# A gated cross-attention and expert layer: order of SyncE's loads around the fourth expert, of VectorE's head splits, and four tiles of TensorE's loop written out

## What is computed

```python
x = x + tanh(g_xattn) * attention(ctx, layernorm(x), mask)   # queries from x; keys, values from ctx and x; 4 heads of 64
x = x + tanh(g_ffn) * experts(layernorm(x))                  # top 2 of 8 experts per token, weighted by router probability
# expert(x) = gelu(x @ w1[e] + b1[e]) @ w2[e] + b2[e]        # w1: 256 x 1024, w2: 1024 x 256
```

## Time and profile before

| | |
|---|---|
| timed runs | 896.8, 899.3, 900.4 us; median 899.3 |
| profiled execution, its own time | 906.47 us |
| its span, first to last instruction | 904.7 us |
| mean granted clock of TensorE | 0.987 |
| PE busy | 855.7 us (95%) |
| DVE busy | 645.3 us (71%) |
| ACT busy | 511.5 us (57%) |
| POOL busy | 289.5 us (32%) |

### The profile page before, as it was taken

How to read it: one execution, slowest core, us unless ns; L and a number is a source line. 1 busy time by engine, 2 the same in 40 slices (tenths; PEclk the granted TensorE clock), 3 DMA queues, 4 the chain that set the end, 5 groups by cost and what they waited for, 6 DMA issues and landing times.

```text
span 904.7 us, 19559 instructions
## 1 busy us (share of the span) xinstructions
PE 855.7 (95%) x5968; PEld 657.3 (73%) x5968; DVE 645.3 (71%) x1500; ACT 511.5 (57%) x1371; POOL 289.5 (32%) x241
## 2 busy tenths in 40 slices
PE   3898999999999999999999999899999999999995
PEld 3654555545555455555469999899999999999995
DVE  6766777768777667676897777775755776676695
ACT  2668875787857877468841843443433443353462
POOL 2321212221265212641054238332332322232233
PEclk8899999999999999999999999999999999999998
DMA  4801000130012201120044649352442535362272
GB/s 128 248 1 50 1 1 1 47 96 1 7 54 82 94 1 56 50 94 1 2 137 99 181 82 259 58 144 47 96 90 43 137 72 114 47 145 45 37 230 27
DMA packets 71896, 70.26 MB, mean 78 GB/s; under 512 B 18593, under 2 KB 66977, under 8 KB 71841
## 3 DMA queue, kind: packets, MB, share of 16 engines
q1 hardware_dynamic: 57696, 52.73, 20.0%
q0 software_dynamic: 13152, 16.86, 10.9%
q10 hardware_dynamic: 992, 0.00, 0.1%
HBM read 44.04 MB, written 26.31 MB: 78 GB/s over the span
## 4 chain that ended last, share of the span: by engine, by line
PE 56%; DVE 17%; issue 13%; POOL 8%; ACT 4%; DMA 1%; another core or an unknown queue 0%; SPq 0%; POOLq 0%; DVEq 0%; ACTq 0%
PE psS L1705 22%; PE psF L1901 10%; PE psO L1901 10%; DVE p_sum L1141 6%; PE psS L1822 4%; POOL rr L681 4%; POOL routed L691 3%; PE psO L1838 3%; PE psF L1705 2%; PE psF L1869 1%; ACT sq L828 1%; DMA xr<-in_x 1%; PE psO L1850 1%; DVE Q L1124 1%; PE psO L1705 1%
## 5 line engine op out<-in xcount | busy, mean ns | idle before, releaser
L889 ACT ACTIVATE V<-psS,b_col 128x256 f32<-128x256 f32 x280 | 116.9, 470 | 214.8 <-PE psS L1705 195.3
L699 POOL DMA_INDIRECT out<-V,token_i x70 | 121.5, 1736 | 261.8 <-DVE V L1332 240.5
L872 ACT ACTIVATE p_ring<-psS,shift 128x1024 f32<-128x1024 f32 x128 | 136.6, 1111 | 71.7 <-PE psS L1822 69.7
L681 POOL TENSOR_TENSOR rr<-ssm,minus_half 128x4 f32<-128x4 f32 (+1 forms) x72 | 76.1, 1057 | 282.4 <-DVE ssm L1105 282.4
L1838 PE MATMUL psO<-p_ring,V 128*64 128x512 f32 x576 | 148.5, 612 | 0.0
L1141 DVE TENSOR_TENSOR p_sum<-p_sum,p_ring 128x1024 f32<-128x1024 f32 (+1 forms) x112 | 135.7, 1211 | 1.3
L1901 PE MATMUL psF<-ln_hi,K 128*128 128x256 f32 x560 | 124.2, 285 | 0.2
L1822 PEld LDWEIGHTS psS<-Q,K 64*128 64x128 f32 x864 | 77.0, 187 | 61.3 <-issue 41.9
L1822 PE MATMUL psS<-Q,K 64*128 64x512 f32 x864 | 121.3, 413 | 0.0
L1901 PE MATMUL psO<-ln_hi,K 128*128 128x256 f32 x560 | 120.5, 279 | 0.0
L1309 DVE CAST K<-V 128x512 fp32r<-128x512 f32 x140 | 60.4, 431 | 59.1 <-ACT V L889 57.0
(11 more groups left out here) (297 smaller groups left out, 1766.5 us busy)
## 6 DMA issues: line engine op xcount, KB each, us to landing
xr<-in_L_ffn_w SPq DMA_DIRECT2D x11, 1024.0 KB, 8.2
xn<-in_L_ffn_w SPq DMA_DIRECT2D x11, 1024.0 KB, 5.6
lnf<-routed SPq DMA_DIRECT2D x35, 258.0 KB
routed<-pad_rows SPq DMA_DIRECT2D x17, 258.0 KB, 9.9
xr<-in_x SPq DMA_DIRECT2D x8, 512.0 KB, 4.5
xb<-in_x SPq DMA_DIRECT2D x4, 1024.0 KB, 6.1
out<-xb SPq DMA_DIRECT2D x4, 1024.0 KB
b_raw<-in_L_ffn_b SPq DMA_DIRECT2D x11, 128.0 KB, 3.5
```

The costliest lines, as they stand in the source:

```text
L681: pool.tensor_tensor(rr[0:p, c % 2, n], ssm[0:p, c % 2, n], minus_half[0:p, n], ALU.pow).then_inc(rr_ready, 1)
L699: pool.indirect_dma_start(out_rows, bass.IndirectOffsetOnAxis(ap=token_i[:, m:m + 1], axis=0), y_out[:, m, :], None, bounds_check=NTOK - 1 ...
L872: act.activation(p_ring[0:p, u % RING, :], psS[u % 2][0:p].rearrange("p a n -> p (a n)"), ACT.Exp, bias=bias).then_inc(exp_done, 1)
L889: act.activation(g32[:, q % 2, (c % 2) * TM:(c % 2 + 1) * TM], psH[q][:, (c % 2) * TM:(c % 2 + 1) * TM], ACT.Gelu_apprx_tanh, bias=b1_col[ ...
```

## The change

On SP, the first weights of expert 3 are sent ahead of the last three pads, and its second weights behind the rows of tile 8 and b1. The wait for the whole plan moves behind the loads for tiles 9 and 10; for the rows one part of the plan is waited for. On DVE, `mean_squares(c)` moves ahead of `heads_lo(c-1)` in the groups with `behind` (not i = 0, not the `waited` ones, not i = 6 of windows 3 and 5). `router_softmax` of windows 3 and 5 (i = 4) moves ahead of `scale_heads`; `norm_offsets` of sequence 1 moves from group 5 to group 4; `plan_experts` moves behind `turned_lo(8)` and `take_meta(8)`. On PE, tiles 5 to 8 are written out and the loop starts at 9.

```diff
                     pad(e)
                 load_rows(7, kept_row(7))
+                load_w1(3)
                 for e in range(5, NE):
                     pad(e)
-                load_w1(3)
-                load_w2(3)
                 load_rows(8, kept_row(8))
                 load_b1(3)
+                load_w2(3)
                 sp.wait_ge(scattered, B * (32 * T))
                 sp.wait_ge(pads_filled, 16 * NE)
-                sp.wait_ge(plan_ready, 4)
+                sp.wait_ge(plan_ready, 1)
                 load_rows(KTILES, sp.value_load(tile_row[0:1, KTILES:KTILES + 1], min_val=0, max_val=NE * REGION - TM))
...
                 load_b1(KE + 1)
+                sp.wait_ge(plan_ready, 4)
                 tiles = sp.value_load(tile_count[0:1, 0:1], min_val=SURE, max_val=NTILES)
...
-                    if turned_at(g) is not None and not waited:
+                    routed = not even and past and not last
+                    behind = tile_at(g) is not None and turned_at(g) is not None and not waited and i != 0 and not (routed and i == 6)
+                    if turned_at(g) is not None and not waited and not behind:
                         heads_lo(turned_at(g))
                     if tile_at(g) is not None:
                         mean_squares(tile_at(g))
+                    if behind:
+                        heads_lo(turned_at(g))
+                    if routed and i == 4:
+                        router_softmax(b - 1)
...
-                    if even and more and b == 0 and i == 5:
+                    if even and more and b == 0 and i == 4:
                         norm_offsets(b + 1)
...
                         if i == 4:
-                            router_softmax(b - 1)
                             router_largest(b - 1, 0)
...
                         activate(t, q)
-                    if t == 7:
-                        plan_experts()
...
                         if t == 7:
+                            plan_experts()
                             plan_switches()
...
-                with pe.Fori(5, SURE - 1) as t:
+                for t in range(5, KTILES):
+                    first_layer(t)
+                    turn_tile(t + 1)
+                    second_layer(t)
+
+                with pe.Fori(KTILES, SURE - 1) as t:
```

## The result

The changed kernel took 902.7 us (median of 7 runs, 901.3 to 904.3), the kernel before beside it 899.9 (7 runs, 896.8 to 900.7). The ratio is 1.0031, with a 95% interval of 1.0017 to 1.0045. I had forecast 899.1 us and no change that can be measured. It is slower by 2.8 us: inside my range, short of my bound of 0.5%, and well outside what the interval leaves to chance. The profiled execution of the changed kernel took 904.25 us, with a span of 902.5.

What follows compares the result with a forecast made beforehand. PE was taken to set the end, so edits count only through gaps between its matmuls. From 899.3 us, attention gains of 6.5, attention losses of 6.9 and 0.6 won in the experts gave 899.1 us, range 892.5 to 904.

Steps and rivals of the forecast that it cites:

- the last term of the sum: Experts, tiles 7 to 10: of 8.5 us lost in the profile, 1.3 left to win in timed runs, half taken: -0.6 us.
- The five long turn waits: Attention: PE's waits of 0.75 to 1.00 us before turning heads each shrink by 0.46 us, 2.3 us gained.
- the offsets: Attention, `norm_offsets` moved to group 4: ready before ACT asks, so the turn in group 7 is no longer late; 1.5 us gained.
- the softmax: Attention, windows 3 and 5: `router_softmax` moves into DVE's wait for POOL's 1.12 us; 0.65 us each, 1.3 us gained.
- i = 8: Attention, windows 2, 4 and 6: DVE's split waits behind `ssm` for ACT's squares, PE's transposes start 1.02 us later each time.
- i = 7: Attention, windows 2, 4 and 6: `ssm` waits for squares, the split PE already waits for starts 0.7 us later each time.
- i = 2 of windows 3 and 5: Attention: `turn_norm` needs a split that now ends later, behind `ssm`; 0.7 us lost each, 1.4 us in all.
- window 7: Attention, i = 1: `turn_logits` loses 0.3 us by the same reckoning as `turn_norm`.
- The second rival: Attention: `heads_lo` comes in time for the extra transposes, so gains stand alone: 892.2 us; chance 0.12.
- the third: Attention: bank waits stay, gains fail because late turns follow DVE's total work; only the offsets' 1.5 us kept: 904.7 us; chance 0.13.
- POOL's scatters bind: Experts, tile 9: the last scatter starts at 571.73, later than the plan would be; if it binds anyway, the edits win nothing.
- The first rival: Experts: tile 7's stall is in the timed runs and the edits end it, 8.5 us less: 891.2 us; chance 0.17.

Runs made afterwards that it cites:

- late heads put back: Changed kernel, but DVE takes the heads' low half in the old order in nine groups of windows 2 to 7; 896.07 us, ratio 0.9951 to the kernel before.
- scatters early: Changed kernel, but POOL sends the last sequence's scatters in two eights ahead of the adds of tiles 5 and 6; 903.05 us, ratio 1.0025 to the kernel before.
- the wait filled: Changed kernel, but PE turns the identity 28 times ahead of its wait for tile 9's rows; 899.83 us, ratio 1.0000 to the kernel before.
- late heads put back, SP's order of before: Changed kernel with the heads' low half in the old order in nine groups and SP's order as before; 893.48 us, ratio 0.9927 to the kernel before.
- late heads put back, wait filled: Changed kernel with the heads' low half in the old order in nine groups and 28 identity turns before tile 9's rows; 893.12 us, ratio 0.9922 to the kernel before.
- the last experiment: Changed kernel, but expert 3's second weights leave ahead of tile 8's rows, as in the kernel before; 900.43 us, ratio 1.0012 to the kernel before.

## Why the prediction was wrong

**The step that failed** is the last term of the sum, "What of the 8.5 us is in a timed run? ... -0.6 us". I took what the edits do in tiles 7 to 10 for a small gain. Less what the attention gained in the profile (0.65 us), they cost about 3.5 us in the first measurement (medians 899.9 and 902.7) and 2.4 in the second (900.4 and 902.1). Two things were left out.

The first is a wait. I had written that "the rows of tile 9 can't be sent before 573 or so, and the turn of tile 9 is due at 575.7", and stopped there. I gave the last scatter only its 1.10 us on POOL; the rows left 4.5 us behind its start, at 576.10, and PE had them another 3.4 us later, where I had put nothing. About a microsecond of this is the change's own: with only some of its parts the rows leave 3.3 to 3.5 us behind that start. So PE, with tiles 7 and 8 undisturbed, came early to rows that come late, and stood 4.37 us. For the most part that is the old loss moved.

The second is the clock. I counted a standstill by its own microseconds and left out what it does to the tile behind it: 2.2 us. The Trainium skill has this mechanism ("TensorE: Matmul & The Clock Gate", section "HAM oscillation — how this bites in real kernels"): a wait for a DMA between bursts of matmuls lowers the clock, and the burst behind it starts slow. The traces here agree: 14.07 us for a tile of 11.84. I had weighed a rule on instruction fetching and not this one, which spoke against the change.

| in the profile, tiles 7 and 8 | longest wait of PE, us | half clock there, us | clock's cost in the timed runs, us |
|---|---|---|---|
| kernel before | 1.6 | 3.4 | 7.7, 7.5 and 7.0 (35, 30, 23 runs) |
| the same, again | 1.6 | none | 8.4 |
| SP's edits alone | 1.2 | none | 8.4 |
| attention edits alone | 0.7 | none | 9.1 |
| all but SP's edits | 0.7 | none | 7.9 |
| written out only | 1.0 | none | 7.6 |
| changed kernel | 4.4 and 4.6 | 6.8 and 6.9 | 10.6 and 9.6 |
| late heads put back | 4.0 | 3.4 | 9.6 |
| scatters early | 1.9 | 3.4 | 10.1 |
| second weights ahead of tile 8's rows | 3.1 | 3.4 | 8.9 |
| the wait filled | 1.6 | none | 6.8 |
| late heads put back, SP's order of before | 1.3 | none | 7.6 |
| late heads put back, wait filled | 1.8 | none | 6.9 |

The last column scatters by half a microsecond and more (the copy of the kernel before stands at 8.4, its runs beside it at 7.7), and the attention edits alone, at 9.1, lie higher than a profile without such a stretch would have it. But the three kernels that have all of SP's edits, the written-out tiles and nothing in the wait (9.6 to 10.6) lie above every other row, and the two with the wait filled lie lowest, level with the kernel before beside them (7.0).

The filled wait takes the half clock away and the ratio back to 1.0000, in the experts about +0.6 us where I had -0.6. So the larger part of the term, 1.5 to 2.8 us, is the clock behind the wait. That rests on the two pairs with the wait filled; in which stretch the clock fell in the timed runs the records don't say, only its mean over the run.

**The attention was right**, item by item, and its sum near enough: -0.65 us in the profile, +0.4 forecast. The five long turn waits shrank by 0.46 to 0.60 us by the spacing (0.46 forecast), the offsets gave 1.49 (1.5), the softmax 0.68 in each window (0.65), i = 8 lost 1.03 (1.02), i = 7 0.69 (0.7), i = 2 of windows 3 and 5 0.71 (0.7), window 7 0.26 (0.3). Gains were 0.9 us larger than I had them. That two sums of 7 us cancel is shown apart by the kernel with the nine groups put back: 6.1 us less. The second rival (waits covered) and the third (gains that don't come) are out: the waits were not covered, and the gains came.

**The experts, point by point.** The wait for `w_lo` is gone from the changed profile, and its worth in timed runs is nothing that shows, as I said of `plan_experts`. The early weights are hidden, as I said; that the rows of tile 8 get out from behind 1 MB is worth 3.1 us, but only where the first weights too stand ahead of the pads (the last experiment), and then only until tile 9. Of the plan's wait I said that it gains nothing because the scatters come later than the plan. In the kernel before they did not: SP sent the rows of tile 9 at 578.89 after 19.8 us on the plan's last part, with no wait for scatters behind it, since DVE was held up with the rest of tiles 7 and 8:

```profile
SPq L614 <- DVE tile_next L1394: 19.8, 1, 19.8
```

That was a row that I could have read. The edit does send these rows 2.8 us earlier, at 576.10, to where the scatters bind; it shows in no timed run, because where DVE isn't held up the whole plan is there by then too (all but SP's edits: the rows leave at 574.54, after 0.6 us on the scatters). "POOL's scatters bind" was right for the turn of tile 9, and wrong as a reason to expect no change: with the scatters ahead of it, DVE's results came late in turn.

The first rival, that the stall of tile 7 is in timed runs and its end gives 8.5 us, is out, though a part of its first half may be true: the loss of tile 7 is in all three profiles with SP's order of before and PE's loop from tile 5, and it ends with SP's edits alone or with the tiles written out alone. It comes back at tile 8 or 9. The Trainium skill's rule ("Runtime: NRT & Kernel Launch", "Instruction fetch mechanics") is not settled by this: writing the tiles out does end tile 7's gaps, as the rule has it, but so does SP's order with the loop in place, and with tiles written out, SP's order of before and the other edits, a gap of the same kind ("issue", 0.7 us) stands in tile 8. What fills those gaps stays open. That the timed runs don't change when they end (0.9999 and 0.9995) has two readings, that the rows of tile 9 would have cost as much anyway, or that most timed runs don't have them; no run here tells these apart.

My reason for -0.6 took the profiled execution's 7.2 us over the median for the stall itself. A part of them was the clock, which stands at 0.987 in the table of the profile before: 906.5 x 0.013 = 11.8 us, against 7.0 to 7.7 a run in the timed ones. For the rest, the profiles give an estimate. In all kernels but the three with the nine groups put back (nine kernels, eleven profiles), the time of the profiled execution less its stretch between the turns of tiles 7 and 11 is 848 to 851 us. A run of the kernel before at its median of 899.9 to 900.4 us then has 49 to 52 us for this stretch, a loss of 2 to 5 us and not of 8.5; at 903.5, in the first set, 52 to 55. By this estimate a good part of the stall that the edits aim at was not in the timed runs at 900 us, and the profiles of before and after, in which the change looks 2.2 us faster (904.7 and 902.5), compare an unusually long tail with a usual one. This is argued from sums; no timed run shows its stretches.

## What to carry to other kernels

- When the last of several late inputs can't be moved, removing the ones ahead of it gathers the loss into one long wait. Price that wait, and ask whether the engine's clock comes through it: here 4.4 us in one piece cost some 2 us of clock, which losses in small pieces did not in seven kernels of eight, and 3.2 us of transposes without use in the wait gave it back.
- Split a change that reorders one engine's work by the places where it acts. Here the edits held 7 us of gains and 7 us of losses, each readable from a row beforehand; leaving out nine groups made the kernel 0.5% faster than the one before, and 0.7 to 0.8% with the clock kept up.
- Compare the mean granted clock of the timed runs, not only their times: it pointed to the cause (0.989 against 0.992) while the profiles' spans pointed the other way (902.5 against 904.7). But it is a pointer and no price: it took a kernel with work in the wait to show the cause.
- Before a stall in a profile is priced, compare the profiled execution with the timed ones. Here the first profile of the kernel before was of an execution slower than all timed ones beside it, and the second was of the slowest of its twelve.

## What the runs showed of the hardware

In these profiles a standstill of TensorE of 1.9 to 4.6 us in one piece in the experts overlaps or is followed by 3.4 to 6.9 us at half clock (four kernels, five profiles). Of the eight other kernels, whose longest wait there is 0.7 to 1.8 us, seven show none and the kernel before shows one in one of two profiles, behind a row of gaps. Twenty-eight matmuls with the identity, 3.2 us of them, kept the clock up through such a wait in two kernels. How the standstill is cut is not all that counts: between the turns of tiles 7 and 10 the kernel with the tiles written out takes 38.16 us and the changed one 42.08; of the difference, 2.5 us are idle time of PE (1.91 and 4.38) and the rest is the half clock's 2.2 (14.06 where the next tile takes 11.84) less small differences in tile 8. From the start of the last scatter to SP's issue of tile 9's rows it took 4.4 to 5.2 us in the six profiles with all of SP's edits and the written-out tiles, and 3.3 to 3.5 us in six profiles with only some of these; why is not shown.
